# The norms' rows, attention 2's probabilities and attention 1's lower exponentials transposed by DMA instead of TensorE

## The reference

```
h = gelu(other @ W[:D] + readout @ W[D:] + b)                      # token projection
y = layernorm(h);  sim = (y @ y.T) / max(|y_i| |y_j|, 1e-8)        # attention 1, no weights
h = h + softmax(sim) @ y + y
x = layernorm(h)                                                   # attention 2, 8 experts
logits = x/|x| @ sim_matrix/|sim_matrix| - sigmoid(gates)
mask = logits > 0, or the two best where none is;  r = softmax of relu(logits) under the mask
q, k, v = sum over experts e of mask[t,e] * (x[t] @ proj[e])       # 256 -> 128
p = softmax(q k.T / sqrt(128)), causal
h = h + sum over e of mask[t,e] r[t,e] * ((p v)[t] @ o_proj[e])
```

## Time and profile before

| | |
|---|---|
| median of 3 runs | 709.59 us (709.16 to 709.88) |
| profiled execution | span 708.6 us, 1.0 us less than the median |
| TensorE busy | 703.0 us, 99% of the span |
| VectorE, ScalarE, GpSimd busy | 81%, 53%, 57% |
| TensorE's granted clock | full in all 40 slices |

### The profile page before, as it was taken

How to read it: one execution, slowest core, us unless ns; L and a number is a source line. 1 busy time by engine, 2 the same in 40 slices (tenths; PEclk the granted TensorE clock), 3 DMA queues, 4 the chain that set the end, 5 groups by cost and what they waited for, 6 DMA issues and landing times.

```text
span 708.6 us, 18356 instructions
## 1 busy us (share of the span) xinstructions
PE 703.0 (99%) x5356; PEld 467.6 (66%) x5356; DVE 572.1 (81%) x1456; ACT 373.1 (53%) x808; POOL 402.7 (57%) x669
## 2 busy tenths in 40 slices
PE   9999999999999999999999999999999999999997
PEld 8888666665757666575756666575766656575655
DVE  5888898887979888787979888787988878786736
ACT  4977373554546364553646355454646356364443
POOL 7642326756466566746566575646556674653434
PEclk9999999999999999999999999999999999999999
DMA  9681230303021030302111030303113020301121
GB/s 242 150 190 48 63 78 6 96 2 86 14 67 33 12 88 0 93 7 73 27 47 52 7 93 0 88 12 67 33 18 81 0 93 7 77 26 53 15 75 30
DMA packets 57975, 39.87 MB, mean 56 GB/s; under 512 B 29928, under 2 KB 53720, under 8 KB 57816
## 3 DMA queue, kind: packets, MB, share of 16 engines
q1 hardware_dynamic: 57552, 39.16, 21.8%
q10 hardware_dynamic: 392, 0.32, 0.2%
HBM read 30.45 MB, written 9.01 MB: 56 GB/s over the span
## 4 chain that ended last, share of the span: by engine, by line
PE 97%; DMA 1%; issue 1%; POOL 0%; ACTq 0%; POOLq 0%; DVE 0%; ACT 0%; DVEq 0%
PE bank L1752 77%; PE bank L1815 7%; PE bank L1669 5%; PE bank L1726 3%; PE bank L1658 2%; PE bank L1886 2%; PE bank L1801 1%; PE bank L1674 1%; DMA region_b<-in_x_dram 1%; PE bank L1837 0%; PE bank L1826 0%; PE bank L1829 0%; POOL region_c L699 0%; POOL region_c L692 0%; PE bank L1706 0%
## 5 line engine op out<-in xcount | busy, mean ns | idle before, releaser
L1752 PE MATMUL bank<-xm,w_qkv 128*128 128x374 f16 x2304 | 415.7, 322 | 0.0
L1752 PEld LDWEIGHTS bank<-xm,w_qkv 128*128 128x128 f16 x2304 | 221.4, 98 | 140.9
L961 ACT ACTIVATE region_c<-bank,out_w 128x256 f32<-128x256 f32 x180 | 85.0, 472 | 170.6 <-PE bank L1752 169.5
L1341 DVE TENSOR_TENSOR xm<-xT,mask_all 128x1496 f16<-128x1496 f16 x128 | 154.6, 1230 | 0.1
L1752 PE MATMUL bank<-w_o,aoT 128*128 128x512 f16 x540 | 143.3, 379 | 0.0
L1245 DVE SCALAR_TENSOR_TENSOR h<-bank,out_w,h 128x256 f32 (+1 forms) x180 | 86.0, 478 | 54.7 <-ACT region_c L961 49.1
L692 POOL TENSOR_TENSOR region_c<-region_c 128x512 f32<-128x512 f32 x46 | 78.5, 1706 | 27.8 <-ACT region_c L961 22.8
L729 POOL TENSOR_TENSOR exp_hl<-exp,exp_hl 128x128 f16<-128x128 f32 (+2 forms) x48 | 34.2, 714 | 83.2 <-ACT exp_hl L903 83.2
L1752 PEld LDWEIGHTS bank<-w_o,aoT 128*128 128x128 f16 x540 | 50.0, 98 | 39.6
L699 POOL TENSOR_TENSOR region_c<-region_c 128x256 f32<-128x256 f32 x46 | 46.9, 1019 | 8.1 <-POOL region_c L692 7.9
L1815 PE MATMUL bank<-xhl,exp_hl 128*128 128x257 f16 (+1 forms) x432 | 50.3, 272 | 0.0
(11 more groups left out here) (205 smaller groups left out, 1059.3 us busy)
## 6 DMA issues: line engine op xcount, KB each, us to landing
mask_all<-d_mask SPq DMA_DIRECT2D x32, 384.0 KB, 4.2
h<-in_x_dram SPq DMA_DIRECT2D x16, 256.0 KB, 4.9
out_dram<-h SPq DMA_DIRECT2D x31, 128.0 KB
rnorm_row<-d_rnorm SPq DMA_DIRECT2D x16, 192.0 KB, 3.9
d_v<-xinT SPq DMA_DIRECT2D x14, 192.0 KB, 4.4
xinT<-d_v SPq DMA_DIRECT2D x56, 48.0 KB, 2.3
h<-in_x_dram SPq DMA_DIRECT2D x15, 112.0 KB, 5.6
out_dram<-h SPq DMA_DIRECT2D x15, 112.0 KB
```

What stands on the lines that cost most here:

```text
L961: a.activation(prod[:, prod_buf(n, t), q, :], pair_bank(n, p)[:, C:2 * C], ACT.Copy, scale=weights_out(n)[:, t, 2 * q + 1:2 * q + 2]).then ...
L1341: v.tensor_tensor(xm[:, e, :, 0:T], xT[1][:, :, :, 0:T].rearrange("p a c t -> p (a c) t"), mask_all[:, e, 0:T].unsqueeze(1).broadcast_to([ ...
L1752: last = t_.matmul(dst, left[lp], right[rp], start=(starts and k == 0), stop=(stops and k == 2), skip_group_check=True)
```

## The change

For batches 2 to 15 (probabilities: batches 0 to 13) the four kinds of transposes leave TensorE, and the copies from PSUM that follow them leave ScalarE and VectorE. In their place SyncE issues seven transposing DMAs a batch from SBUF to SBUF, through the DMA crossbar: one for norm 1's rows (both halves, 12 blocks, 384 KB), two for norm 2's (6 blocks each, 192 KB), two for the lower exponentials (3 blocks each, 96 KB), two for the probabilities (7 blocks each, one of them unused, 224 KB). The batches of the prologue and the probabilities of batches 14 and 15 stay on TensorE.

The tiles are laid out in blocks of 128x128 for it; norm 1's high half, which `attend` reads with a column of sums, is therefore written twice by ScalarE (`xh_sum` is the second). The lists are reordered: in SyncE's step the exponentials', the probabilities' and norm 2's transfers come first, norm 1's goes between v out and v in, the stores stay last. TensorE does units 5 and 6 ahead of `attend`, two units of k (16, 17) early, 8 to 10 between `probs_v` and the first pair, `logits` after pair 2, and unit 15 (the last of v) after `turn_mask` and pair 4. GpSimd does `low_1` behind the first sum of products. Some buffers of the setup share space with `exp2`, and several semaphores become one (`s_passed`). The core of the diff:

```diff
-    PT_OFF = [sum(TP - P * jj for jj in range(j)) for j in range(NT)]
+    PT_OFF = [NT * P * j for j in range(NT)]
+    PT_BLOCKS = NT + (NT - 1) * (NT - 1)
...
-        xhl = [sb(f"xhl{n}", [P, 2, NT, C + 2 * (2 - n)], F16) for n in (1, 2)]
+        xs = [part(region_b, n * NT * C, NC, NT, P) for n in (0, 1)]
+
+        xhl = [sb(f"xhl{n}", [P, 2, NC, NT, P], F16) for n in (1, 2)]
+        xh_sum = sb("xh_sum", [P, NT, C + 2], F16)
...
-        exp1_hl = sb("exp1_hl", [P, 2, NT, TP], F16)
+        exp1 = part(region_a, NT * TP, NT, TP)
+        exp1_hl = sb("exp1_hl", [P, 2, NT * (NT + 1) // 2, P], F16)
+        exp1_lower = sb("exp1_lower", [P, 2, NT * (NT - 1) // 2, P], F16)
...
+        def exp1_row(p, t):
+
+            return exp1_hl[:, p, ROW_AT[t]:ROW_AT[t] + ROW_STEP[t] * (NT - 1 - t) + 1:ROW_STEP[t], :]
+
+        def exp1_block(p, j, t):
+
+            if j <= t:
+                return exp1_hl[:, p, ROW_AT[j] + ROW_STEP[j] * (t - j), :]
+            return exp1_lower[:, p, {(1, 0): 0, (2, 0): 1, (2, 1): 2}[j, t], :]
+
+        def as_blocks(ap):
+
+            return ap.rearrange("p (b q) -> p b q", q=P)
+
+        def probs_tile(p, i):
+
+            return exp2_hl[:, p, :].rearrange("p (k q) -> p k q", q=P)[:, i:i + (NT - 1) * i + 1:NT - 1, :]
...
+            def first_rows_around(g):
+
+                sp.wait_ge(s_hi1, 2 * (g + 1)).then_inc(s_passed, 1)
+                sp.wait_ge(s_lo1, g + 1).then_inc(s_passed, 1)
+                sp.wait_ge(s_dots_done, NT * g).then_inc(s_passed, 1)
+                sp.dma_start_transpose(xT[0][:, :, :, :].rearrange("p a c (t q) -> p (a c t) q", q=P),
+                                       xhl[0][:, :, :, :, :].rearrange("p a c t q -> p (a c t q)")).then_inc(s_T1_moved, 16)
...
+            def exponentials_around(f):
+
+                sp.wait_ge(s_att_done, NT * f).then_inc(s_passed, 1)
+                for p, done in enumerate((s_exp1_hi, s_exp1_lo)):
+                    sp.wait_ge(done, NT * f + NT - 1).then_inc(s_passed, 1)
+                    sp.dma_start_transpose(exp1_lower[:, p, :, :],
+                                           exp1_hl[:, p, ABOVE, :].rearrange("p b q -> p (b q)")).then_inc(s_exp1_moved, 16)
+
+            def probs_around(n):
+
+                sp.wait_ge(s_exp2_hi, NT * (n + 1)).then_inc(s_passed, 1)
+                if later(n):
+                    sp.wait_ge(s_pv_done, n).then_inc(s_passed, 1)
+                for p in range(2):
+                    if p == 1:
+                        sp.wait_ge(s_exp2_lo, n + 1).then_inc(s_passed, 1)
+                    sp.dma_start_transpose(pT[:, p, :].rearrange("p (k q) -> p k q", q=P),
+                                           exp2_hl[:, p, :]).then_inc(s_pT_moved, 16)
+
+            def second_rows_around(f):
+
+                for p, done in enumerate((s_hi2, s_lo2)):
+                    sp.wait_ge(done, f + 1).then_inc(s_passed, 1)
+                    if p == 0:
+                        sp.wait_ge(s_xm_ready, E * f).then_inc(s_passed, 1)
+                        sp.wait_ge(s_logits_done, f).then_inc(s_passed, 1)
+                    sp.dma_start_transpose(xT[1][:, p, :, :].rearrange("p c (t q) -> p (c t) q", q=P),
+                                           xhl[1][:, p, :, :, :].rearrange("p c t q -> p (c t q)")).then_inc(s_T2_moved, 16)
...
             def step(i, g, f, m, n):
+                if f is not None and not early(m):
+                    exponentials_around(f)
+                if n is not None and by_trip(n):
+                    probs_around(n)
                 if early(m):
                     load_output_weights()
                     mask_around(f)
+                if f is not None and not early(m):
+                    second_rows_around(f)
                 if g is not None:
                     norms_out(g)
                     norms_in(g)
                 if f is not None and not early(m):
                     mask_around(f)
                 if m is not None and by_trip(m):
-                    values_around(m)
+                    values_out(m)
+                if g is not None:
+                    first_rows_around(g)
+                if m is not None and by_trip(m):
+                    values_in(m)
...
-                    add_tile(n, 0)
-                if g1 is not None and not early(m):
-                    low_1(g1)
+                    sum_products(n, 0)
+                    if g1 is not None:
+                        low_1(g1)
+                    sum_halves(n, 0)
+                    add_sum(n, 0)
...
+            def high_1(b):
+                act.wait_ge(s_xs1, NT * (b + 1))
                 if later(b):
-                    act.wait_ge((s_att_done, s_turned2_hi)[n], (NT, 1)[n] * b)
-                a.activation(xhl[n][:, 0, :, 0:C], xs[n][:, :, :], ACT.Copy).then_inc((s_hi1, s_hi2)[n], 1)
+                    act.wait_ge(s_att_done, NT * b)
+                a.activation(xhl[0][:, 0, :, :, :], xs[0][:, :, :, :], ACT.Copy).then_inc(s_hi1, 1)
+                a.activation(xh_sum[:, :, 0:C].rearrange("p t (c q) -> p c t q", c=NC), xs[0][:, :, :, :],
+                             ACT.Copy).then_inc(s_hi1, 1)
...
                     dve.wait_ge(s_k_done, E * (b - 1) + e + 1)
+                    if e == 0 and by_trip(b - 1):
+                        dve.wait_ge(s_v_done, b)
...
-                turned = as16(turn[1], NC * TP).rearrange("p (a w) -> p a w", a=2)
-                for j in range(1, NT):
-                    at = sum(range(1, j)) * P
-                    v.tensor_copy(exp1_hl[:, :, j, 0:j * P], turned[:, :, at:at + j * P]).then_inc(s_exp1_square, 1)
+                v.tensor_copy(exp1_lower[:, :, :, :].rearrange("p a b q -> p (a b q)"),
+                              as16(turn[1], NC * TP)).then_inc(s_exp1_square, 1)
...
                     exp_low(f, 2)
-                    exp_lower(f)
                     mask_scores(n, 2, out_bank[0])
                     mask_tokens(m, E - 2)
                     mask_tokens(m, E - 1)
                     residual(f)
-                    turned_probs_low(n)
...
                     head_low(qT, qkv_bank[0], s_q_hi, m + 1, s_q_lo, qkv_out)
-                    turned_low_2(f)
                     pairs(0, 2)
...
+                if t == 0 and isinstance(f, int) and f < 2:
+                    pe.wait_ge(s_T1, 2 * (f + 1))
+                elif t == 0:
+                    pe.wait_ge(s_T1_moved, 16 * (f - 1))
                 if t == 0:
-                    pe.wait_ge(s_T1_hi, f + 1)
...
+                if t == first and isinstance(f, int) and f < 2:
+                    pe.wait_ge(s_exp1_square, f + 1)
+                elif t == first:
+                    pe.wait_ge(s_exp1_moved, 32 * (f - 1))
                 for j in range(NT):
-
-                    for k, (ep, xp, n) in enumerate(((0, 0, C + 1), (0, 1, C), (1, 0, C + 1))):
-                        last = t_.matmul(banks[t][:, 0:n], exp1_hl[:, ep, j, t * P:(t + 1) * P],
-                                         xhl[0][:, xp, j, 0:n], start=(j == 0 and k == 0),
-                                         stop=(j == NT - 1 and k == 2), skip_group_check=True)
+                    high, low = (exp1_block(p, j, t) for p in range(2))
+                    t_.matmul(banks[t][:, 0:C + 1], high, xh_sum[:, j, 0:C + 1], start=(j == 0), stop=False,
+                              skip_group_check=True)
+                    t_.matmul(banks[t][:, 0:C].rearrange("p (c q) -> p c q", c=NC), high, xhl[0][:, 1, :, j, :],
+                              start=False, stop=False, skip_group_check=True)
+                    last = t_.matmul(banks[t][:, 0:C + 1], low, xh_sum[:, j, 0:C + 1], start=False, stop=(j == NT - 1),
+                                     skip_group_check=True)
                 last.then_inc(s_att_done, 1)
...
             def probs_v(n):
-                pe.wait_ge(s_pT_hi, n + 1)
-                pe.wait_ge(s_pT_lo, n + 1)
                 if by_trip(n):
+                    pe.wait_ge(s_pT_moved, 32 * (n + 1))
                     pe.wait_ge(s_v_tok_ready, 2 * (n + 1))
                 else:
+                    pe.wait_ge(s_pT_hi, n - LAST_TRIP)
+                    pe.wait_ge(s_pT_lo, n - LAST_TRIP)
                     pe.wait_ge(s_v_tok_ready, 2 * (LAST_TRIP + 1) + n - LAST_TRIP)
...
-                    M(*range(13, 22))
-                    turn_first_high(g1)
-                    M(22)
-                    turn_first_low(g1)
-                    M(23)
+                    M(*range(13, 24))
                     return
 
                 if f is not None and n is not None:
...
                     score(n, 0)
                     score(n, 1)
                     M(4)
-                    turn_exp(f)
                     score(n, 2)
-                    pe.wait_ge(s_T1_hi, f + 1)
-                    M(5)
+                    M(5, 6)
                     for t in range(NT):
                         attend(f, t)
-                    M(6)
```

(44 more changed lines are left out.)

315 lines of the change are left out of this document (157 added, 158 removed).

## The result

The changed kernel takes **755.16 us** (median of 4 runs, 747.54 to 757.38) against 709.71 us: ratio 1.062, interval 1.059 to 1.065. It is slower by 45 us, where 713 us was predicted, in a range of 690 to 735. The profiled execution took 757.2 us and has a span of 755.4.

A forecast was written before the change was run, and what follows sets the result against it. TensorE's matmul list bounded the kernel; its saved 32.6 us would return as waits on a closed chain. 709.6 + 4.5 (13 periods, 40.7 instead of 40.35) + 0 (head) - 1.1 (end) = 713 us, range 690 to 735.

The forecast's parts named there:

- a chain through attention 1, routing, GpSimd's sums, the last store and the exponentials' transfers: Loop of batches: this chain closes on itself, making the period 40.7 instead of 40.35 us, +4.5 us in all.
- From the last store to the landing, 3.2 us: SyncE's queue: last store issued at 37.5, low half leaves at 37.9 after 0.4 issue, lands 2.8 later at 40.7.
- the rival of slow transfers: SyncE's queue: issue about 1 us or 96 KB landing in 4 us or more; 723 up, about 735, upper 750; chance 0.22.
- Landing, 2.8 and 3.4 us: Transposing transfers: 2.8 us to land for 96 KB, 3.4 for 192 KB, with ends 2.2 and 4.4 for both.
- Waits for heads and mask: TensorE waits 0.7 us for the heads before the first pair and 0.3 us for the mask.
- The copy of v in front of the routing exponential: ScalarE's queue: v's copy starts at 6.05 after the logits instead of 5.28, moving GpSimd's start from 21.85 to 22.4.
- Unit 6 ahead of attention 1, at nothing a period: TensorE's list: one unit ahead adds 0.95 us before the first attention and removes 0.95 after the last.
- Stores out of the way give 0.4 us a period: SyncE's queue: without the stores the low half could leave at about 37.5, giving back only some 0.4 us.
- Clock: TensorE: read as at full clock in every slice of the kernel before; no term for a slower clock.
- TensorE's busy time, about 670 us: Whole kernel: TensorE's busy time should fall to about 670 us, from 703.0.
- Head, 0: Up to the first attention: transposes save 0.67 and 0.33 us, one unit ahead adds 0.95, net 0.
- From the last attention to the end, -1.1 us: After the last attention: 1.34 of transposes and 0.95 of unit go, waits 0.7 and 0.3 and 0.2 of transposes come.

The follow-up runs named there:

- the kernel of 708.90 us: Changed kernel, all transfers kept, with late store, one exponentials' transfer, unit 6 behind attention 1, batch 2's rows on TensorE, unit 15 ahead of mask: 708.90 us (0.9991).
- the kernel of 698.09 us: Changed kernel with exponentials and batch 2's first rows on TensorE, unit 6 behind attention 1, unit 15 ahead of mask, pair 5 behind pair 4: 698.09 us (0.9832).

## Why the prediction was wrong

The direction held, and so did the mechanism: a chain through attention 1, routing, GpSimd's sums, the last store and the exponentials' transfers, of which the shorter list of TensorE gives nothing back. The size failed: 42 us too little. Two periods of after, counted from attention 1's start: one at full clock (from 197.66, next 240.34), and one that begins at half clock (from 329.02, next 373.36). Their rows of VectorE, GpSimd and SyncE's queue:

```profile
200.90 0.15 DVE L1474 RECIPROCAL inv_sum<-bank 118x1 f32<-118x1 f32 x1
...
333.91 0.15 DVE L1474 RECIPROCAL inv_sum<-bank 118x1 f32<-118x1 f32 x1
...
339.72 0.96 DVE L1493 TENSOR_TENSOR xhl<-region_b,xhl 128x768 f16<-128x768 f32 x1 [1.01 <-ACT xhl L924]
```
```profile
220.73 1.27 POOL L776 TENSOR_TENSOR region_c<-region_c 128x512 f32<-128x512 f32 x1 [0.34 <-ACT region_c L1061]
...
353.74 1.27 POOL L776 TENSOR_TENSOR region_c<-region_c 128x512 f32<-128x512 f32 x1 [0.34 <-ACT region_c L1061]
...
366.74 1.02 POOL L790 TENSOR_TENSOR h<-region_c,h 128x256 f32 x1 [0.36 <-POOL region_c L783]
```
```profile
235.56 0.30 SPq L581 DMA_DIRECT2D out_dram<-h  x1
236.59 2.55 SPq L552 DMA_TRANSPOSE exp_lower<-exp_hl  x2
```

| | predicted | full clock | begins at half clock |
|---|---|---|---|
| VectorE takes the third tile | 3.2 | 3.24 | 4.89 |
| low rows 2 ready | 9.9 | 10.01 | 11.66 |
| GpSimd's first sum starts | 22.4 | 23.07 | 24.72 |
| its last addition ends (14.0 us of work in all three) | 36.4 | 37.09 | 38.74 |
| last store issued | 37.5 | 38.20 | 39.86 |
| first transfer's issue begins | 37.5 | 38.93 | 40.59 |
| second's begins | 37.9 | 40.30 | 41.96 |
| second has landed: the period | 40.7 | 42.7 | 44.3 |

- **From the last store to the landing, 3.2 us (0.4 for an issue, 2.8 for the landing): wrong, the step that failed.** It took 4.5. The queue takes 0.73 us from the store to the first transfer across the loop's return, which had no term (0.36 where the last step is written out: 672.55 to 672.91). From the first transfer's issue to the second's it is 1.37 us, not 0.4, for an issue is 1.2 us whatever the size. The landing gives 0.4 back. "If issuing a transposing transfer takes about 1 us" was in the rival of slow transfers, with a chance of 0.22; the forecast had taken its issue from a row of a plain store. That rival's upper end, 750, came from landings of 4.4 us, which no run shows, and the measured time lies above even this.
- **Landing, 2.8 and 3.4 us: right.** 2.4, 2.8 and 2.9 us for 3, 6 and 7 blocks, so rows 2 just come in time, as said (0.7 us of wait for them in all).
- **Waits for heads and mask: right** (0.7 and 0.3 predicted; 0.81 and 0.21). The copy of v in front of the routing exponential was seen, and priced as 0.55 us on GpSimd's start (21.85 to 22.4). At full clock that start came 0.7 us later still, with the logits 0.25 late; undone, the copy's place gave 0.84 us a period.
- **Unit 6 ahead of attention 1, at nothing a period: wrong too, but hidden here.** The prediction counted the unit as TensorE's time, once added and once taken off, and never asked when VectorE has expert 6's tokens. The row of before was there to be read. VectorE makes the last two experts' tokens from 347.02 to 349.28, so expert 6's are there at about 348.2 (an estimate, half of the row); attention 1, from 347.15, covers the wait:

```profile
347.02 2.26 DVE L1341 TENSOR_TENSOR xm<-xT,mask_all 128x1496 f16<-128x1496 f16 x2
```

  In the changed kernel attention 1 waits 1.12 us more for the transfer after unit 6, so the table's terms add up to the period without it. It is the next limit, close behind: 41.37 us a period with the store late, 41.75 with the exponentials on TensorE, both above the predicted 40.7. Alone it costs 18 us. What its return alone gives in the changed kernel, no run shows.
- **Stores out of the way give 0.4 us a period: wrong.** It was 24 us in all, the half clock among them. The 0.4 held for an issue of 0.4, when the low half decides. With 1.37 from one issue to the next the queue has to begin as soon as the high half is there: in the run with the late store it begins 37.2 after attention 1's start (316.49), in the changed kernel at full clock 38.93.
- **Clock: not foreseen.** Full in every slice before, it was taken as given. Six periods and 1.65 us each make the difference between 42.7 and 44.3.
- **TensorE's busy time, about 670 us: wrong.** It is 698.9 us. In part that is the half clock, which makes matmuls longer (0.42 us instead of 0.27 in attention 1) in seven stretches; with all transfers and full clock (the kernel of 708.90 us) it is 677.1.
- **Head, 0: wrong.** Attention 1 of batch 2 starts 6.9 us later. By the differences between the runs 4.1 of them are batch 2's first rows, for whose transfer TensorE has no other work and after which it runs at half clock for some 3 us, and 2.2 are unit 6:

```profile
101.06 2.10 PE L1842 MATMUL bank<-xT 128*128 128x384 f16 x6 [2.79 <-DMA xT<-xhl]
...
112.05 0.27 PE L1908 MATMUL bank<-xh_sum,exp_hl 128*128 128x257 f16 x1
```

- **From the last attention to the end, -1.1 us: wrong, and small.** It is 78.7 us (676.75 to 755.4), 0.2 less than before (629.72 to 708.6).

The sum of the profiled execution: 713 + 13 x 2.0 (period at full clock) + 6 x 1.65 + 6.9 + 0.9 = 757, where it took 757.2.

The runs show 1.2 us of issue for a transfer of three to seven blocks, and the plain store was issued in 0.30; 96 KB landed in 2.4 us, plain 48 KB in 2.3. The price that the Trainium skill gives for the crossbar (VectorE: DVE Perf Modes, "The three transpose paths", 1309 ns for 128x128) is therefore no price per block here: six blocks are issued in 1.29 us and have landed after 2.8. Its rule, TensorE where PSUM will do (same page, "Rules for kernel authors"), is borne out for the exponentials alone; the kernel of 698.09 us gains by moving the others. That such transfers are as fast as plain ones, as the Trainium skill has it (Advanced Engine Details and Errata, "X-Bar Transpose (TRN2)"), agrees with the landings of the runs and not with their issue.

Not settled: why the half clock comes in six of eleven like places; how much of the period of 39.2 us, 0.9 over TensorE's own list of some 38.3 (40.35 - 36 x 0.056), can still be had; and whether the 0.7 us across the loop's return is the jump or the waits behind it.

## What to carry to other kernels

A transfer may take the place of an engine's work only where its issue, its landing and everything queued ahead of it fit between producer and consumer: norm rows and probabilities had microseconds to spare and gained 11 us (698.09 against 709.62, with the lists in the order of that run), the exponentials, last made and first needed, lost as much again for 0.33 us of transposes. Before moving any unit, ask when each of its operands is made, not only how long it takes. And once a full engine begins to wait, look at its clock over a few us at a time, not in the page's slices.

## What was not expected of the hardware

- A transposing transfer between SBUF buffers holds SyncE's queue 1.18 to 1.25 us, with 3, 6 or 7 blocks of 128x128 (1.29 for the six in one); the one of 12 blocks 1.45 us at the median:

```profile
L480 SPq DMA_TRANSPOSE xT<-xhl x14: 1289/1450/1782, 96.2 to 660.5; - x14
```

- Such blocks land fast: 3.8 us (median) for 384 KB, where a plain transfer of 192 KB to memory takes 4.4.
- After waits of 0.40, 0.71 and 1.12 us close behind each other TensorE was granted 1.2 GHz for some 3 us in six of the eleven attentions before which they stood, with matmuls of 256 columns 0.215 us apart instead of 0.11. Useless matmuls in the last wait kept it at 2.4 GHz in all of them in the profiled execution. The same came after the one wait of 2.79 us ahead of batch 2's first rows; in the kernel with the useless matmuls that wait was 2.42 us, and the clock stayed up.
